# Where the last group of tokens is normalised for the last MLP

## What is computed

```python
ln_out = layernorm(hidden_states, ln1_s, ln1_b)
ctx = merge_heads(attention(split_heads(q), split_heads(k), split_heads(v), ltor_mask))
x = hidden_states + (ctx @ w_ao + b_ao)
ln_out = layernorm(x, ln2_s, ln2_b)
ctx = merge_heads(attention(split_heads(q), split_heads(k), split_heads(v), cross_mask))
x = x + (ctx @ w_co + b_co)
ln_out = layernorm(x, ln3_s, ln3_b)
mlp_out = gelu(ln_out @ w1 + b1) @ w2 + b2
return x + mlp_out
```

## Time and profile before

| | |
|---|---|
| median of 3 runs | 1772.55 us (1770.03 to 1774.36) |
| the profiled execution | 1772.42 us |
| its span, first to last instruction | 1770.7 us |
| PE busy | 1672.8 us (94%) |
| PE weight load busy | 1437.8 us (81%) |
| ACT busy | 979.1 us (55%) |
| DVE busy | 891.6 us (50%) |
| POOL busy | 543.4 us (31%) |
| mean granted TensorE clock | 0.975 of full speed |

### The profile page before, as it was taken

How to read it: one execution, slowest core, us unless ns; L and a number is a source line. 1 busy time by engine, 2 the same in 40 slices (tenths; PEclk the granted TensorE clock), 3 DMA queues, 4 the chain that set the end, 5 groups by cost and what they waited for, 6 DMA issues and landing times. The chain is left out here.

```text
span 1770.7 us, 35569 instructions
## 1 busy us (share of the span) xinstructions
PE 1672.8 (94%) x14356; PEld 1437.8 (81%) x14356; DVE 891.6 (50%) x1680; ACT 979.1 (55%) x1868; POOL 543.4 (31%) x602
## 2 busy tenths in 40 slices
PE   7999999999999999999999799899989799987699
PEld 5899999999989999999999789676666567766598
DVE  6543333333354333333334364577769566767432
ACT  4445554555455455545554355467658577776444
POOL 5211010101143010001001071267744487776311
PEclk9999999999999999999999999899989899999699
DMA  6040000000000000000000000300010000001001
GB/s 179 14 123 24 0 24 24 24 0 24 25 1 25 25 24 0 24 24 24 0 24 1 11 21 1 105 2 2 2 22 1 7 1 2 1 13 31 1 12 36
DMA packets 59133, 40.01 MB, mean 23 GB/s; under 512 B 15725, under 2 KB 58262, under 8 KB 59030
## 3 DMA queue, kind: packets, MB, share of 16 engines
q1 hardware_dynamic: 57414, 37.78, 7.4%
q10 hardware_dynamic: 1616, 0.79, 0.2%
HBM read 36.46 MB, written 2.10 MB: 22 GB/s over the span
## 5 line engine op out<-in xcount | busy, mean ns | idle before, releaser
L629 ACT ACTIVATE l0a_q<-l0a_q_ps,l0a_head_bias 128x512 f32<-128x512 f32 x128 | 88.4, 690 | 330.4 <-PE l0a_q_ps L83 330.4
L830 DVE TENSOR_TENSOR l0a_c_lo<-l0a_c_ps,l0a_c_hi 128x512 fp32r<-128x512 f32 x64 | 44.3, 692 | 278.5 <-ACT l0a_c_hi L682 278.5
L326 POOL TENSOR_TENSOR l0a_w_lo<-l0a_raw,l0a_w_hi 128x512 fp32r<-128x512 f32 x32 | 41.8, 1307 | 446.5 <-ACT l0a_w_hi L600 446.5
L840 DVE TENSOR_TENSOR x<-l0a_o_ps,x 128x1024 f32<-128x1024 f32 x64 | 78.3, 1224 | 162.6 <-PE l0a_o_ps L83 127.5
L81 PE MATMUL l0a_v_ps<-l0a_wv_hi,ctx_hi 128*128 128x256 f32 x512 | 149.9, 293 | 0.0
L81 PE MATMUL l0a_o_ps<-l0a_wo_hi,l0a_c_hi 128*128 128x256 f32 x512 | 148.8, 291 | 0.7 <-DVE l0a_c_lo L830 0.7
L82 PE MATMUL l0a_v_ps<-l0a_wv_lo,ctx_hi 128*128 128x256 f32 x512 | 143.9, 281 | 0.0
L82 PE MATMUL l0a_o_ps<-l0a_wo_lo,l0a_c_hi 128*128 128x256 f32 x512 | 143.8, 281 | 0.0
L83 PE MATMUL l0a_o_ps<-l0a_wo_hi,l0a_c_lo 128*128 128x256 f32 x512 | 143.7, 281 | 0.0
L83 PE MATMUL l0a_v_ps<-l0a_wv_hi,ctx_lo 128*128 128x256 f32 x512 | 143.6, 280 | 0.0
L633 ACT ACTIVATE l0a_k<-l0a_kt_ps,l0a_head_bias 128x512 f32<-128x512 f32 x128 | 88.2, 689 | 62.8 <-PE l0a_kt_ps L83 62.4
(11 more groups left out here) (435 smaller groups left out, 4921.6 us busy)
## 6 DMA issues: line engine op xcount, KB each, us to landing
l0a_raw_v<-in_L_xattn_wv_dram SPq DMA_DIRECT2D x16, 256.0 KB, 3.2
l0a_raw_o<-in_L_xattn_wo_dram SPq DMA_DIRECT2D x32, 128.0 KB, 2.7
l3a_room<-in_L_xattn_wo_dram SPq DMA_DIRECT2D x2, 2048.0 KB, 8.7
l0a_raw<-in_L_xattn_wq_dram SPq DMA_DIRECT2D x31, 128.0 KB, 2.3
l0a_raw<-in_L_xattn_wk_dram SPq DMA_DIRECT2D x31, 128.0 KB, 2.3
x<-in_x_dram SPq DMA_DIRECT2D x4, 512.0 KB, 8.1
l3a_room<-in_L_xattn_w_fc_dram SPq DMA_DIRECT2D x2, 1024.0 KB, 6.6
l3a_room<-in_ctx_dram SPq DMA_DIRECT2D x1, 2048.0 KB, 10.4
```

The source lines that it names most:

```text
L326: return pool.tensor_tensor(w[p][1][:], raw[p][:], w[p][0][:].bitcast(F32), ALU.subtract)
L629: act.activation(q[p][:], q_ps[:], ACT.Identity, bias=head_bias[p][:, 0:1]).then_inc(q_done, 1)
L830: dve.tensor_tensor(c[p][1][:], attended[p][:], c[p][0][:].bitcast(F32), ALU.subtract).then_inc(c_lo, 1)
L840: dve.tensor_tensor(chip.x[:, own, :], o_ps[:], chip.x[:, own, :], ALU.add).then_inc(added, 1)
```

## The change

In the attention stage the pairs 14 and 15 are no longer normalised: `normed_pair` gives none for them, and the stage has one slot less. Their `bn_stats` stay. The MLP gets the gain as `late`: at its start DVE gathers the last group's four tiles, POOL makes 1/deviation and normalises the four tiles, at step f = 5 of the first group PE turns them with eight transposes into two PSUM banks of their own, and at step 6 ACT, DVE and POOL make `h_hi`, the whole value and `h_lo` of the last group. The first product of the last group waits for `late_lo`. PE's groups are now written out and not looped; ACT's and DVE's loops stay.

```diff
-def dense_mlp(chip, tag, function, prepared, out=None, turn=None, entry=None):
+def dense_mlp(chip, tag, function, prepared, out=None, turn=None, entry=None, late=None):
...
+        if late is not None:
+            LATE = 5
+            last_rows, last_columns = slice((NG - 1) * GT, NG * GT), slice((NG - 1) * GN, NG * GN)
+            late_spread, late_inverse = sb("late_spread", [P, GT]), sb("late_inverse", [P, GT])
+            late_rows, late_whole = sb("late_rows", [P, GT, D]), sb("late_whole", [P, CH, GN])
+            late_ps = chip.ps(f"{tag}_late_ps", [P, CH, GN], stack)
...
@@ POOL, ahead of its groups @@
+                if late is not None:
+                    pool.wait_ge(late_gathered, 1)
+                    pool.tensor_scalar(late_spread[:], chip.x_moments[:, last_rows, 1], 1e-5, None, ALU.add).then_inc(late_spread_done, 1)
+                    pool.wait_ge(late_spread_done, 1)
+                    pool.tensor_tensor(late_inverse[:], late_spread[:], chip.minus_half[:].to_broadcast([P, GT]),
+                                       ALU.pow).then_inc(late_inverse_done, 1)
+                    pool.wait_ge(late_inverse_done, 1)
+                    for t in range(GT):
+                        at = last_rows.start + t
+                        pool.tensor_scalar(late_rows[:, t, :], chip.x[:, at, :], chip.x_moments[:, at, 0:1], late_inverse[:, t:t + 1],
+                                           ALU.subtract, ALU.mult).then_inc(late_rows_done, 1)
@@ POOL, behind the bias of group 0 @@
+                    if late is not None and g == 0:
+                        for c in range(CH):
+                            pool.wait_ge(late_whole_done, c + 1)
+                            pool.tensor_tensor(chip.h_lo[:, c, last_columns], late_whole[:, c, :], chip.h_hi[:, c, last_columns].bitcast(F32),
+                                               ALU.subtract).then_inc(late_lo, 1)
@@ PE @@
+                    if late is not None and f == 0 and isinstance(g, int) and g == NG - 1:
+                        pe.wait_ge(late_lo, CH)
...
+                def turn_late():
+                    for c in range(CH):
+                        for j in range(GT):
+                            if c == 0:
+                                pe.wait_ge(late_rows_done, j + 1)
+                            last = pe.transpose(late_ps[:, c, j * P:(j + 1) * P], late_rows[:, j, c * P:(c + 1) * P], chip.ident[:])
+                        last.then_inc(late_turned, 1)
...
+                        if late is not None and isinstance(g, int) and g == 0 and f == LATE:
+                            turn_late()
...
-                if turn:
-                    for g in range(NG - 1):
-                        group(g, True)
-                else:
-                    with pe.Fori(0, NG - 1) as g:
-                        group(g, True)
+                for g in range(NG - 1):
+                    group(g, True)
@@ ACT, behind the hidden block of step 6 @@
+                    if late is not None and f == LATE + 1:
+                        for c in range(CH):
+                            act.wait_ge(late_turned, c + 1)
+                            act.activation(chip.h_hi[:, c, last_columns], late_ps[:, c, :], ACT.Identity,
+                                           bias=late[:, 1, c:c + 1], scale=late[:, 0, c:c + 1]).then_inc(late_hi, 1)
@@ DVE, behind the low part of step 6, and at the stage's start @@
+                        if late is not None and isinstance(g, int) and g == 0 and f == LATE + 1:
+                            for c in range(CH):
+                                dve.wait_ge(late_hi, c + 1)
+                                dve.tensor_scalar(late_whole[:, c, :], late_ps[:, c, :], late[:, 0, c:c + 1], late[:, 1, c:c + 1],
+                                                  ALU.mult, ALU.add).then_inc(late_whole_done, 1)
...
+                if late is not None:
+                    for t in range(last_rows.start, last_rows.stop):
+                        last = dve.bn_aggr(chip.x_moments[:, t, :], chip.x_stats[:, t, :])
+                    last.then_inc(late_gathered, 1)
@@ narrow_attention @@
-        return t // 2 if t is not None and t % 2 == 1 and (t < TILES - NT or following) else None
+        return t // 2 if t is not None and t % 2 == 1 and (t < TILES - NT or following and t < TILES - GT) else None
-    SLOTS = CHUNKS + LAG + (6 if ending else 3 if following else 2)
+    SLOTS = CHUNKS + LAG + (6 if ending else 2)
@@ all_layers @@
-        dense_mlp(chip, "l3m", ACT.Gelu_apprx_tanh, beside["finished"](dict(place=place)), out)
+        dense_mlp(chip, "l3m", ACT.Gelu_apprx_tanh, beside["finished"](dict(place=place)), out,
+                  late=beside["gain"])
```

3 lines of the change are left out of this document (added).

## The result

| | before | after |
|---|---|---|
| median of ten runs | 1772.47 us (1768.76 to 1774.99) | 1762.59 us (1758.66 to 1766.78) |
| the profiled execution | 1772.42 us | 1762.88 us |
| its span | 1770.7 us | 1761.2 us |
| mean granted clock | 0.975 | 0.979 |

The ratio is 0.9944, with a 95% interval of 0.9934 to 0.9954: 0.56% faster, where 0.3% can be told. 1763.8 was predicted.

A forecast was written before the change was run, and what follows sets the result against it. PE, never idle, bounds the last MLP; the attention stage ends in a chain of short passes with PE idle. Terms of -7.10, -2.74, +0.3 and +0.80 gave -8.74 us, so 1763.8 us, range 1761.0 to 1766.4.

The forecast's parts named there:

- 1, pair 15: End of the last attention stage: everything between the last statistics and the last h_lo pass's end goes, gain 7.10 us.
- 2, pair 14: Last attention tile: without this pair's turns and passes, output product and addition come earlier, gain 2.74 us.
- 3, GpSimd meets DVE: Attention stage's end: GpSimd's earlier ctx_lo passes delay DVE's h_lo pass of pair 13, loss 0.3 us.
- 4, eight turns: Last MLP's first group: eight added transposes on PE, loss 0.80 us.
- 5, waits in the MLP: Last MLP's first group: PE's added waits are met, rows ready by 10.7 us after the start; loss nothing.
- 6, slow start: Last MLP's start: 5.26 us at 1.2 GHz stays despite the shorter pause, no change.
- One of my own signs: Last MLP's start: prediction wrong if the first matmul, forecast near 1664.6, does not come at least 9 us earlier.
- Rival A: Last MLP's start: clock stays at 2.4 GHz over the shorter pause, 2.6 us more gain, 1761.2; chance 0.11.
- Rivals B and D: B: GpSimd holds DVE beyond one pass, 1766.0, chance 0.13; D: something hidden sets attention's end, half the gain, 1768.7, 0.04.

The follow-up runs named there:

- e_pair15: Against before: only pair 15 moved to the MLP (two tiles, four turns), pair 14 stays in the attention stage; 1765.47 us, ratio 0.9964.
- e_unroll: Before with PE's groups of the last MLP written out and nothing else; 1774.14 us, ratio 1.0006.
- e_sbuf: Before with four unused SBUF tiles taken ahead of the last MLP's hidden buffers; 1773.12 us, ratio 0.9997.
- e_hold: After with GpSimd's last two ctx_lo passes held until DVE's h_lo pass of pair 13 is done; 1762.45 us, ratio 0.9944 to before.
- e_both: Against before: the attention stage keeps its pairs and the MLP normalises the last group again; 1774.66 us, ratio 1.0010.
- e_moved: After with its four new SBUF tiles taken behind the hidden buffers; 1764.13 us, ratio 0.9948 to before.
- e_late3w: After with the last three groups normalised in the MLP, and ten unread transposes on PE; 1757.86 us, ratio 0.9908 to before.
- e_warm: After with ten unread transposes on PE at the attention stage's end; 1761.07 us, ratio 0.9927 to before.

## Why the prediction was right, and which of its steps were off

The total was within 1.2 us of the median. What the change removes was read rightly: counted from the start of l3a, l3m comes 9.5 us earlier between the means of five and of three kernels, where terms 1 to 3 give 9.54. In the two profiled executions alone the picture is less clean: two terms fell short, and three amounts that I hadn't counted made up for it, two of them scatter or possibly so. That the parts come out even there is luck. By the steps of the prediction, in these two executions (a plus is time lost):

| step | predicted | found | from |
|---|---|---|---|
| 1, pair 15 | -7.10 | -7.10 | e_pair15; boundary 1.04 for 1.05 in after |
| 2, pair 14 | -2.74 | -2.16; at equal clock -2.85 (high) and -2.62 (low) | start of o_t_lo to the last addition: 4.40 before, 4.86 in e_unroll and e_sbuf; 2.24 after, 1.55 in e_hold |
| 3, GpSimd meets DVE | +0.3 | +1.27, 0.96 of it clock | o_t_lo 0.77 later, from a stage 0.5 ahead |
| 4, eight turns | +0.80 | +0.79, and 0.10 in the step behind | 1683.88 to 1684.67; e_both |
| 5, waits in the MLP | 0 | 0 | no PE idle time; rows ready after 7.55 us |
| 6, slow start | 0 | -1.2 | six slow gaps fewer |
| not foreseen: steps | | -0.7 | e_sbuf, e_moved |
| scatter ahead of the last slots | | -0.5 | GpSimd's mask pass at 1639.39, before 1639.89; no edit there: l3a began 1.30 later and then got here 1.8 sooner |

The found terms sum to 1.27 + 0.79 + 0.10 - 7.10 - 2.16 - 1.2 - 0.7 - 0.5 = -9.5.

One of my own signs failed: I wrote that the prediction is wrong if the MLP's first matmul does not come at least 9 us earlier, and it came 8.49 earlier. The last statistics ended at 1664.65 and not near 1663.6. Counted from the start of l3a it is 9.79 us, so it failed by what scattered ahead of the stage, and a sign within half a microsecond of the forecast, read in one execution, was too tight to test the mechanism.

**Terms 1 and 4** held, with nothing to add. **Term 2** was right in mechanism: in e_hold, where the last product runs at 2.4 GHz, the addition comes 1.55 us behind o_t_lo's start, and I had 1.66. In after it ran at 1.2 GHz, which the step "without them the addition follows the product as tile 30's did" left out. Before's own tail ran at the high clock; against e_unroll and e_sbuf, whose old tail ran as slowly as that of after, the gain is 4.86 - 2.24 = 2.62 us. So the missing 0.58 is mostly the clock of two executions and not the pair.

**Term 3** named the right meeting and nearly the right length: DVE was held by 0.68 us, through one pass and not both. The starts and lengths fit: a first GpSimd pass of 1.25 us from 1653.82 ends at 1655.07, the h_lo pass ends 0.59 later at 1655.66, and a second GpSimd pass of 1.14 then ends at 1656.80, where the two passes' 2.98 us end. The rule of the Trainium skill (SBUF — State Buffer, Who interferes with whom) that was read there with one pass agrees with this row. What I missed is the other input of that turn on PE. DVE's addition was over at 1656.61 and PE came at 1657.10, late by its own slow turns. Of the 1.27 us, 0.70 are the eight turns and 0.26 the step behind them (1.90 from that turn to the product, 1.64 before), all PE at half clock; 0.31 were lost before tile 29's product, which began at 1653.95, only 0.19 us ahead of before (1654.14), and I did not trace them. With the turns at the high clock PE would have come 0.19 us earlier than in the earlier trace rows, at 1656.40, and waited for DVE to 1656.61 + 0.15 = 1656.76: 0.36 us, about what I put there. As it was, the hold hid behind the clock, and the 0.96 us of clock are not the change's doing as far as the runs show, since e_unroll and e_sbuf have the same slow turns without it.

**Term 5**: the bound of 10.7 us for the rows was 7.55, since the operations on four columns take 0.23 and 1.04 us and not a whole pass. GpSimd's passes did hold one low part, at 1676.41, to 0.92 us, without any effect on PE.

**Term 6** is where the reading by the nearest row failed. I took the slow stretch to be 5.26 us whatever happened ahead of it, because l3a had it so behind its pause of 1.87 us. That row was one draw. In the fourteen profiles, with the same instructions ahead and the same pause, l3a reached the high clock after 3.12 to 5.65 us in eight (3.12 in after), and in the other six, e_late3w shown above among them, it began at the high clock and fell back after three matmuls. At the start of l3m the table has 13, 13, 13, 8 and 8 slow gaps in the five kernels with the old end and its pause of 3.86 to 3.87 us, 14 in e_pair15 (3.89), and 7, 7, 7, 8 and 12 behind one of 2.04. So the stretch varies from execution to execution by 1.0 us with nothing changed ahead of it, and the gain of 1.2 us in after may be chance; the shorter pause may have a part in it, which these single executions don't settle. Rival A, the clock up from the start, didn't happen here, but e_warm shows that it was near: ten transposes in PE's waits bring it about. The same section of the Trainium skill as in the prediction (TensorE: Matmul & The Clock Gate, What's actually happening) also says that the number of cold matmuls at a kernel's start differs between runs of one kernel. The 8 to 13 gaps of the five kernels agree, though theirs is a start in the middle of a kernel; with that rule the price of the slow start would have had a range of a microsecond ahead of time and not one value.

Rivals B and D don't show: DVE was held through one pass, tile 31's addition waits for PE, and nothing hidden took the removed chain's place.

## What to carry to other kernels

A stage that ends in a chain of short passes with TensorE idle, next to a stage that TensorE fills, is the place to move work across: here 9.3 us of chain (7.10 and 2.16 in the two traces) became 0.9 us of turns. Cost it pass by pass on the chain, and check the queue of the engine that prepares the moved work, since beyond two groups that queue turned the gain into waits of PE. Then look at the clock on both sides of the boundary: ten transposes that nobody reads, in waits that are there anyway, took away the slow start in all three kernels that have them (90.78 us for the MLP against 92.12), and the ratio went from 0.9944 to 0.9927 with overlapping intervals, where a better order of GpSimd's passes brought nothing. And before a difference between two traces is put down to the change, look at a stage that the change can't touch: here the start of l3a alone moved by 6 us between profiles.

## What the runs showed of the hardware that I had not expected

- The 8 us of scatter between the ten runs of after go roughly with the mean granted clock: 1758.66 and 1758.94 us at 0.981, 1759.90 at 0.980, 1759.64 and 1762.88 at 0.979, 1762.30 and 1762.96 at 0.978, 1765.28 and 1766.78 at 0.976, 1765.72 at 0.975. That scatter is nearly as large as the change (9.9 us); a single run of each would have told little.
- l3m began at 1.2 GHz behind every pause of 2.04 us or more, and at 2.4 GHz in all three kernels with a pause of 1.50 us behind five transposes. The pause and the work ahead of it changed together, so which of the two decides stays open. l3a, behind one and the same pause of 1.87 us, began at 1.2 GHz in eight of fourteen profiles and at 2.4 GHz in six, so the pause alone doesn't decide it there.
- The place of a few tiles in SBUF changed a matmul group's mean from 282 to 279 ns (output part of a step 1.43 to 1.41 us), steadily through the stage, though their contents and shapes and the order were the same.
- In e_late3w four waits of under 1 us each, within 4 us in which PE was busy for 1.4, were followed by half the clock: the matmuls behind them come 0.43 us apart, from 1681.80 on.
